# Keys and values from f16 parts of the context, and the query bias in one product, in a four-layer cross-attention kernel

## The chip, the cores and the metric

The kernel runs on one core of a Trainium2 chip. Its time is the device time of one launch in microseconds (us), and a verdict compares the medians of several runs of both kernels on the same chip.

## What is computed

Eight batches of 100 queries of width 128 go through four layers in turn. Layers 0, 1 and 3 are cross-attention of the queries over the same context of 1444 rows of width 128 (16 heads of 8 columns); layer 2 is causal attention over the first 100 context rows with a feed-forward behind it. Cut to what matters:

```python
# layer 0 (context first normalised by rows and scaled by gkv), layers 1 and 3 alike but with biases
q = (x @ Wq + bq).reshape(B, 100, 16, 8)
k = (ctx @ Wk + bk).reshape(B, 1444, 16, 8)
v = (ctx @ Wv + bv).reshape(B, 1444, 16, 8)
p = softmax(einsum('bshd,bkhd->bhsk', q, k) / sqrt(8))
x = norm(residual + einsum('bhsk,bkhd->bshd', p, v) ...)
```

Layer 0 has no bias of the queries; layers 1, 2 and 3 have one. All inputs are f32.

## The kernel before

**Units and stages.** A unit is one layer of 0, 1, 3 for one batch: 24 units, in the order layer 0 batches 0 to 7, layer 1, layer 3. The program is a pipeline of stages, and in stage n five units are at work: unit n+3 is loaded (`load`), the keys and queries of unit n+2 are made (`prep`), unit n+1 has its values made and the maxima of its scores taken (`top`), unit n has its exponentials and their products with the values (`exp`), and unit n-1 is finished (`post`). Layer 2 of a batch is done in the stages in which layer 3 of the same batch is `load` (attention, `att2`) and `prep` (feed-forward, `ff2`). `Unit.par` is the batch modulo 2, the half of a double buffer.

**Steps.** A stage has 48 steps j, one for each of 12 chunks of 120 or 121 context rows times 4 groups of heads. In each step TensorE makes one score product for the exponentials (L689, f16, 400 columns, into one of three `sexp` banks), one for the maxima (L650, the same shape, into one of four `ring` banks), and every four steps the products of four steps of probabilities with the values (L709). ScalarE takes the exponential (L957), VectorE the running maximum (L1081; L1079 for a first chunk). Every other piece of work is placed at a fixed step by the table `AT`: context transposes ct0 to ct2 at 0, 3, 6 (layer 0 alone), keys k0 to k2 at 9, 12, 15, queries at 19, values v0 to v2 at 22, 24, 26, mask transposes at 28, 30, 32, transposes of the maxima at 36 and 37. Each takes a ring bank in turn, so TensorE waits when the bank's last content hasn't been read. Every engine works strictly in its own written order.

**The work around the change.** `ctf` holds the transposed context in f32, [128, 2, 1444], one half for each parity. In layer 0 TensorE transposes the normalised rows (L577) and ScalarE scales and copies them into `ctf` (L890); in layers 1 and 3 SyncE loads a transposed copy of the context into it (L369), once the values of the unit that used this half are made. The keys are one f32 product of 480 or 484 columns for each of three groups (L588, `wk` stationary), read twice by ScalarE (L903: `kf` in f32, and the high part of `kp` in f16), and GpSimd subtracts the two for the low part (L476). The values are four f32 products of 128 columns in each of three groups (L596, `ctf` stationary, 120 or 121 columns of weights, `wv` moving), copied by ScalarE (L914). The queries are four f32 products of 100 columns (L622), and for layers 1 and 3 each is followed by a product of one row, `bq` with a row of ones, that adds the bias (L624). ScalarE then rounds them to f16 (L945), VectorE makes the parts (L1068), and GpSimd spreads them over heads (L503).

**GpSimd's order** in a stage: `spread2` of layer 2 (L487), three low parts of the keys (L476), `root` (L482), squares of a loaded context (L512, layer 0), `spread` (L503), the normalising of the loaded context (L519, L523, layer 0), and layer 2's `less_maximum` (L494) and `root`.

## Time and profile before

| | |
|---|---|
| median of 3 runs | 1166.34 us (1160.42 to 1167.5) |
| the profiled execution, its own time | 1159.32 us |
| its span, first to last instruction | 1157.5 us |
| busy: TensorE, VectorE, ScalarE, GpSimd | 1054.8, 812.2, 761.9, 292.2 us |
| mean granted TensorE clock | 0.95 of 2.4 GHz |

The span is what the profile's views divide; the profiled execution's own time is 1.8 us longer. Busy time of TensorE (PE) is modelled with overlapping ends, so what a matmul costs is read from the chain of work, where each piece has the time until the next could start; PEld is the loading of weights. DVE is VectorE, ACT ScalarE, POOL GpSimd, SPq the queue that issues DMAs.

### The profile page before, as it was taken

Reading aid. Unit: us, or ns where it says so; the run is one execution under the profiler, and the core shown is the slowest. Engines: PE = TensorE matmul, PEld = TensorE weight load, DVE = VectorE, ACT = ScalarE, POOL = GpSimd, SP = SyncE. Lnnn points to the kernel's source line nnn. Section 1 sums busy time; section 2 is a strip of 40 time slices with the busy share of each in tenths; the row PEclk is TensorE's granted clock in tenths of the full one; section 3 lists DMA queues with packets and bytes.
Section 4 is the critical chain, followed back from the end, with each engine's and each line's share of the span. In section 5 each row is a group of like instructions: output and inputs, shape, how many; then the busy total and the mean of one; then the engine's idle time right before and its main releaser. Section 6 shows DMA issues by size and latency. Waiting matters only on the chain.

```text
span 1157.5 us, 24776 instructions
## 1 busy us (share of the span) xinstructions
PE 1054.8 (91%) x9410; PEld 597.1 (52%) x9410; DVE 812.2 (70%) x1681; ACT 761.9 (66%) x1692; POOL 292.2 (25%) x267
## 2 busy tenths in 40 slices
PE   2689999999899999999999999999989999999996
PEld 1345555555455555555555555555555555564542
DVE  5787778768657767777876667676767777766851
ACT  1266776677577776867774666666666666756676
POOL 5644333532121122012113040404040313221100
PEclk9779999999999999999998899989899989998999
DMA  7421321221222222222231211112120202121100
GB/s 201 107 73 53 85 74 51 66 78 44 80 65 76 72 78 67 76 70 81 77 84 43 66 40 56 45 50 65 31 74 24 80 18 80 34 63 52 29 4 4
DMA packets 64350, 72.81 MB, mean 63 GB/s; under 512 B 8187, under 2 KB 59899, under 8 KB 64104
## 3 DMA queue, kind: packets, MB, share of 16 engines
q1 hardware_dynamic: 64232, 71.22, 21.6%
q8 instruction: 76, 1.25, 0.4%
q14 instruction: 42, 0.34, 0.1%
HBM read 50.25 MB, written 18.15 MB: 59 GB/s over the span
## 4 chain that ended last, share of the span: by engine, by line
PE 68%; DVE 16%; ACT 8%; issue 4%; SPq 1%; POOL 1%; DMA 0%; ACTq 0%; POOLq 0%; DVEq 0%
PE acc L709 17%; PE ring L650 15%; PE sexp L689 15%; PE ring L596 5%; PE ring L588 4%; DVE mx L1081 4%; DVE mneg L1087 4%; DVE mx L1079 3%; PE ring L622 2%; ACT probs L957 2%; PE ring L624 2%; PE ring L773 2%; ACT kp L903 2%; SPq L457 1%; PE ring L577 1%
## 5 line engine op out<-in xcount | busy, mean ns | idle before, releaser
L1081 DVE TENSOR_TENSOR mx<-ring,mx 120x400 f16<-120x400 f32 (+1 forms) x1056 | 556.2, 568 | 220.6 <-PE ring L650 217.3
L957 ACT ACTIVATE probs<-sexp 120x400 f32<-120x400 f32 (+1 forms) x1152 | 540.7, 514 | 191.5 <-PE sexp L689 186.6
L650 PE MATMUL ring<-qx,krep 96*128 96x400 f16 (+2 forms) x1152 | 399.1, 351 | 38.6 <-ACT kp L903 14.2
L689 PE MATMUL sexp<-qx,krep 97*128 97x400 f16 (+2 forms) x1152 | 396.3, 348 | 8.2 <-ACT probs L957 4.5
L709 PE MATMUL acc<-probs,vx 120*18 120x200 f32 (+1 forms) x4608 | 262.6, 347 | 0.8 <-ACT probs L957 0.7
L689 PEld LDWEIGHTS sexp<-qx,krep 97*128 97x128 f16 (+2 forms) x1152 | 126.3, 111 | 150.0 <-ACT probs L957 84.8
L650 PEld LDWEIGHTS ring<-qx,krep 96*128 96x128 f16 (+2 forms) x1152 | 128.5, 112 | 133.9 <-DVE mx L1081 31.0
L476 POOL TENSOR_TENSOR kp<-kf,kp 128x480 f16<-128x480 f32 (+1 forms) x72 | 80.9, 1130 | 357.3 <-ACT kp L903 357.3
L709 PEld LDWEIGHTS acc<-probs,vx 120*18 120x18 f32 (+1 forms) x4608 | 108.7, 99 | 118.6 <-issue 84.1
L503 POOL TENSOR_TENSOR qx<-qs,headmask 96x400 f16<-96x400 f16 x96 | 79.9, 862 | 78.7 <-DVE qs L1068 44.0
L914 ACT COPY vx<-ring 120x512 f32<-120x512 f32 (+1 forms) x72 | 42.3, 587 | 68.2 <-PE ring L596 68.2
L596 PE MATMUL ring<-wv,ctf 128*120 128x128 f32 (+1 forms) x576 | 81.3, 285 | 0.6 <-DVE qs L1068 0.6
L596 PEld LDWEIGHTS ring<-wv,ctf 128*120 128x120 f32 (+1 forms) x576 | 71.3, 187 | 19.8 <-issue 11.5
L588 PE MATMUL ring<-ctf,wk 128*128 128x484 f32 (+1 forms) x144 | 74.2, 600 | 4.2 <-ACT kp L903 2.4
L482 POOL TENSOR_TENSOR rstd<-vare,half 100x1 f32<-100x1 f32 x24 | 13.0, 541 | 215.1 <-DVE vare L1098 215.1
L1079 DVE CAST mx<-ring 121x400 f16<-121x400 f32 x96 | 52.2, 567 | 11.8 <-PE ring L650 11.8
L487 POOL TENSOR_TENSOR kbd<-k,heads 128x1600 f32<-128x1600 f32 x8 | 22.9, 2864 | 141.5 <-ACT v L978 141.5
L1087 DVE TENSOR_REDUCE mneg<-ring 100x8 f16<-100x968 f16 x48 | 55.4, 1156 | 0.9 <-PE ring L665 0.9
L1068 DVE SCALAR_TENSOR_TENSOR qs<-qh,headmask,ring 96x400 f16<-96x400 f16 x24 | 15.0, 627 | 47.6 <-ACT qh L945 47.6
L903 ACT ACTIVATE kf<-ring,cols 128x480 f32<-128x480 f32 (+1 forms) x48 | 31.9, 665 | 12.1 <-PE ring L588 12.1
L945 ACT CAST qh<-ring 96x400 f16<-96x400 f32 x24 | 11.7, 487 | 40.5 <-PE ring L624 36.5
L577 PE MATMUL ring<-ident,nat 120*128 120x120 f32 (+1 forms) x96 | 16.9, 312 | 20.4 <-DMA causal<-in_causal 20.4
(123 smaller groups left out, 924.3 us busy)
## 6 DMA issues: line engine op xcount, KB each, us to landing
krep<-kept SPq DMA_DIRECT2D x144, 120.0 KB, 2.6
ctf<-in_ctxT SPq DMA_DIRECT2D x16, 722.0 KB
kept<-kp SPq DMA_DIRECT2D x48, 240.0 KB, 2.8
krep<-kept SPq DMA_DIRECT2D x72, 121.0 KB, 2.8
kept<-kp SPq DMA_DIRECT2D x24, 242.0 KB, 2.5
nat<-in_ctx SPq DMA_DIRECT2D x8, 720.0 KB
maskexp<-maskmax SPq DMA_DIRECT2D x8, 281.2 KB, 3.4
anymask<-in_mask SPq DMA_DIRECT2D x1, 1128.1 KB, 6.8
```

Of the source, the lines that this page charges most:

```text
L476: pool.tensor_tensor(dst[:, 1, c0:c0 + n], src[:, c0:c0 + n], dst[:, 0, c0:c0 + n], ALU.subtract).then_inc(sem[done], 1)
L503: last = pool.tensor_tensor(qx[0:PARTS, u.third, t, :, :], qs[:, t, :].unsqueeze(1).broadcast_to([PARTS, HT, S]), headmask16[:, :].unsquee ...
L588: pe.matmul(ps[:, 0:n], wk[:, u.L, :], ctf[:, u.par, c0:c0 + n], start=True, stop=True).then_inc(sem["k_filled"], 1)
L596: last = pe.matmul(ps[0:r, D * i:D * i + D], ctf[:, u.par, c0:c0 + r], wv[:, u.L, :], start=True, stop=True)
L650: last = pe.matmul(ps[0:n, 0:QW], krep[0:PARTS, u.par, t, c0:c0 + n], qx[0:PARTS, u.third, t, :, :].rearrange("p f s -> p (f s)"), start=T ...
L689: last = pe.matmul(ps[0:n, 0:QW], krep[:, u.par, t, c0:c0 + n], qx[:, u.third, t, :, :].rearrange("p f s -> p (f s)"), start=True, stop=no ...
L709: last = pe.matmul(acc[32 * q:32 * q + VW, 2 * S * side:2 * S * side + 2 * S], vx[0:r, u.par, PAIRS * c + 2 * t + p, :], probs[0:r, j % PR ...
L903: op = act.activation(dst, src, ACT.Identity, bias=cols[:, bk:bk + 1]) if u.L else act.copy(dst, src)
L957: act.activation(probs[0:r, j % PR, :], sexp[j % SR][0:r, 0:QW], ACT.Exp).then_inc(sem["probs_ready"], 1)
L1079: op = dve.tensor_copy(dst, src)
L1081: op = dve.tensor_tensor(dst, src, dst, ALU.max)
L1087: dve.tensor_reduce(mneg[:, 8 * i:8 * i + 8], bank(f"mt{i}", u)[0:S, :].bitcast(F16).rearrange("s (h n) -> s h n", h=8)[:, :, 0:chunk(0)[1 ...
```

## The change

`ctf` becomes a single buffer [128, 1444]. A new tile `ct` [128, 2, 2, 1444] in f16 holds, for each parity, the high and the low part of the transposed context. GpSimd makes them, three groups per unit, ahead of everything else that it does in a stage: a copy f32 to f16, a wait for it, and a subtraction. Keys become three f16 products for each group (high by high, high weight by low context, low weight by high context), values three for each chunk, each product with its own load of weights. `wk` and `wv` are split once, by VectorE, at the start. The bias of the queries is one f16 product of 400 columns and 36 rows ahead of the four f32 products, which accumulate onto it. The load of the transposed context now waits for the last low part of the unit in `prep`, instead of the values of the unit in `top`. One more constant is loaded (`which`, [36, 401]), and `bq` grows from 1 to 36 rows.

```diff
-        bq = sb("bq", [1, 4, T * PARTS])
-        ones_row = sb("ones_row", [1, S])
+        bq = sb("bq", [32 + T, 4, PARTS])
+        bq16 = sb("bq16", [32 + T, 4, PARTS], F16)
+        which = sb("which", [32 + T, QW + 1])
+        which16 = sb("which16", [32 + T, QW], F16)
...
-        ctf = sb("ctf", [128, 2, KEYS])
+        ctf = sb("ctf", [128, KEYS])
+        ct = sb("ct", [128, 2, 2, KEYS], F16)
...
             def load_transposed(u, before):
 
-                sp.wait_ge(*at("v_filled", before, 3))
-                sp.dma_start(ctf[:, u.par, :], ctxT_in[u.batch]).then_inc(sem["ctx_loaded"], 16)
+                sp.wait_ge(*at("ct_low", before, 3))
+                sp.dma_start(ctf[:, :], ctxT_in[u.batch]).then_inc(sem["ctx_loaded"], 16)
...
                 if s.load is not None and s.load.L:
-                    load_transposed(s.load, s.top)
+                    load_transposed(s.load, s.prep)
...
+            def context(u, g, before):
+
+                _, c0, n, _ = groups()[g]
+                pool.wait_ge(*(at("ct_read", u, g + 1) if u.L == 0 else at("ctx_loaded", u, 16)))
+                if g == 0 and before is not None:
+                    pool.wait_ge(*at("v_filled", before, 3))
+                pool.tensor_copy(ct[:, u.par, 0, c0:c0 + n], ctf[:, c0:c0 + n]).then_inc(sem["ct_high"], 1)
+                pool.wait_ge(*at("ct_high", u, g + 1))
+                pool.tensor_tensor(ct[:, u.par, 1, c0:c0 + n], ctf[:, c0:c0 + n], ct[:, u.par, 0, c0:c0 + n], ALU.subtract
+                                   ).then_inc(sem["ct_low"], 1)
...
             def stage(s, n):
+                if s.prep is not None:
+                    for g in range(3):
+                        context(s.prep, g, s.exp)
                 if s.att2 is not None:
                     spread2(s.att2)
...
             def keys(u, g):
 
-                if u.L == 0:
-                    pe.wait_ge(*at("ct_read", u, g + 1))
-                elif g == 0:
-                    pe.wait_ge(*at("ctx_loaded", u, 16))
+                if u is UNITS[0] and g == 0:
+                    pe.wait_ge(sem["wk_ready"], 1)
+                pe.wait_ge(*at("ct_low", u, g + 1))
                 ps = begin(f"k{g}", u)
                 _, c0, n, _ = groups()[g]
-                pe.matmul(ps[:, 0:n], wk[:, u.L, :], ctf[:, u.par, c0:c0 + n], start=True, stop=True
-                          ).then_inc(sem["k_filled"], 1)
+                for j, (w, c) in enumerate(((0, 0), (0, 1), (1, 0))):
+                    last = pe.matmul(ps[:, 0:n], wk16[:, w, u.L, :], ct[:, u.par, c, c0:c0 + n], start=(j == 0),
+                                     stop=(j == 2))
+                last.then_inc(sem["k_filled"], 1)
 
             def vals(u, g):
 
+                if u is UNITS[0] and g == 0:
+                    pe.wait_ge(sem["rest_ready"], 1)
                 ps = begin(f"v{g}", u)
                 for i, c in enumerate(groups()[g][0]):
                     c0, r = chunk(c)
-                    last = pe.matmul(ps[0:r, D * i:D * i + D], ctf[:, u.par, c0:c0 + r], wv[:, u.L, :], start=True, stop=True)
+                    for j, (w, p) in enumerate(((0, 0), (1, 0), (0, 1))):
+                        last = pe.matmul(ps[0:r, D * i:D * i + D], ct[:, u.par, p, c0:c0 + r], wv16[:, w, u.L, :],
+                                         start=(j == 0), stop=(j == 2))
                 last.then_inc(sem["v_filled"], 1)
...
                 ps = begin("q", u)
+                if u.L:
+                    pe.matmul(ps[0:PARTS, 0:T * S], bq16[:, u.L, :], which16[:, :], start=True, stop=False, skip_group_check=True)
                 for t in range(T):
-                    last = pe.matmul(ps[0:PARTS, S * t:S * t + S], wq[:, u.L, t, :], xT[:, :], start=True, stop=not u.L)
-                    if u.L:
-                        last = pe.matmul(ps[0:PARTS, S * t:S * t + S], bq[0:1, u.L, PARTS * t:PARTS * t + PARTS], ones_row[0:1, :],
-                                         start=False, stop=True)
+                    last = pe.matmul(ps[0:PARTS, S * t:S * t + S], wq[:, u.L, t, :], xT[:, :], start=not u.L, stop=True,
+                                     skip_group_check=u.L > 0)
                 last.then_inc(sem["q_filled"], 1)
...
                 if g == 0 and before is not None:
-                    act.wait_ge(*at("v_filled", before, 3))
-                act.mul(ctf[:, u.par, c0:c0 + n], bank(f"ct{g}", u)[:, 0:n], cols[:, COLC["gkv"]:COLC["gkv"] + 1]
+                    act.wait_ge(*at("ct_low", before, 3))
+                act.mul(ctf[:, c0:c0 + n], bank(f"ct{g}", u)[:, 0:n], cols[:, COLC["gkv"]:COLC["gkv"] + 1]
                         ).then_inc(sem["ct_read"], 1)
...
+            def split(w, high, low):
+                step(dve.tensor_copy(high, w))
+                return dve.tensor_tensor(low, w, high, ALU.subtract)
+
+            split(wk[:, :, :], wk16[:, 0], wk16[:, 1]).then_inc(sem["wk_ready"], 1)
...
-            dve.tensor_scalar(bq[0:1, :, :], bq[0:1, :, :], SCALE, None, ALU.mult)
-            dve.memset(ones_row[0:1, :], 1.0)
+            step(dve.tensor_scalar(bq[:, :, :], bq[:, :, :], SCALE, None, ALU.mult))
+            step(dve.tensor_copy(bq16[:, :, :], bq[:, :, :]))
+            dve.scalar_tensor_tensor(out=bq16[:, :, :], in0=bq16[:, :, :], scalar=which[:, QW:QW + 1], in1=bq[:, :, :],
+                                     op0=ALU.mult, op1=ALU.add)
+            dve.tensor_copy(which16[:, :], which[:, 0:QW])
...
+            split(wv[:, :, :], wv16[:, 0], wv16[:, 1])
```

## Rows read from the trace of the kernel before

**Rows 1.** The page's chain that ended last, share by engine, then by line.
```profile
PE 68%; DVE 16%; ACT 8%; issue 4%; SPq 1%; POOL 1%; DMA 0%; ACTq 0%; POOLq 0%; DVEq 0%
PE acc L709 17%; PE ring L650 15%; PE sexp L689 15%; PE ring L596 5%; PE ring L588 4%; DVE mx L1081 4%; DVE mneg L1087 4%; DVE mx L1079 3%; PE ring L622 2%; ACT probs L957 2%; PE ring L624 2%; PE ring L773 2%; ACT kp L903 2%; SPq L457 1%; PE ring L577 1%
```
**Rows 2.** The chain in a layer-1 stage: start, length (us), engine, line.
```profile
533.62 0.81 PE ring L588 x2
...
535.51 0.56 ACT kp L903
...
537.75 0.17 PE ring L622 x2
537.93 0.34 PE ring L624 x2
538.26 0.34 PE ring L622 x2
...
542.25 1.06 PE ring L596 x8
...
543.48 0.17 PE ring L650
...
544.00 0.88 PE ring L596 x8
...
548.11 0.22 PE ring L605 x4
...
549.88 0.35 PE ring L605 x4
```
**Rows 3.** The chain in a layer-0 stage, at the queries.
```profile
132.38 0.69 PE ring L622 x8
```
**Rows 4.** The chain in a layer-3 stage.
```profile
672.33 0.56 ACT kp L903
...
674.98 0.88 PE ring L794 x8
...
693.73 1.06 PE ring L596 x8
```
**Rows 5.** Groups by line: count, busy us, mean ns, idle before and releasers.
```profile
L476 POOL TENSOR_TENSOR kp<-kf,kp 128x480 f16<-128x480 f32 (+1 forms) x72 | 80.9, 1130 | 357.3 <-ACT kp L903 357.3
L945 ACT CAST qh<-ring 96x400 f16<-96x400 f32 x24 | 11.7, 487 | 40.5 <-PE ring L624 36.5 <-PE ring L622 4.0
L605 PEld LDWEIGHTS ring<-identb,maskb 100*120 100x120 bf16 (+1 forms) x96 | 8.3, 134 | 4.4 <-issue 2.6 <-ACT maskmax L926 0.3
L1107 DVE TENSOR_TENSOR xall<-xn,rows 100x128 f32<-100x128 f32 x8 | 6.1, 759 | 0.3
L548 POOL MEMSET vx<- 128x1728 f32 x2 | 3.1, 1538 | 0.1
L1107 DVE TENSOR_TENSOR att<-xn,rows 100x128 f32<-100x128 f32 x8 | 2.3, 291 | 0.3
L1240 DVE TENSOR_TENSOR xall<-xall,rinvx 100x1024 f32<-100x1024 f32 x1 | 1.2, 1224 | 0.5 <-POOL rinvx L556 0.5
```
**Rows 6.** Windows: busy PE, PEld, DVE, ACT, POOL, then granted clock, DMA.
```profile
132.00:138.00 6.00, 6.00 (x56) 4.30 (x54) 3.79 (x8) 4.01 (x9) 5.99 (x6) 1.00 0.38 106
...
335.00:339.00 4.00, 4.00 (x29) 2.00 (x27) 2.07 (x4) 1.61 (x4) 2.89 (x4) 0.57 0.06 19
...
417.00:421.00 4.00, 4.00 (x38) 2.51 (x38) 2.13 (x5) 2.08 (x5) 2.11 (x3) 1.00 0.25 70
...
547.40:552.60 5.20, 5.20 (x62) 2.97 (x60) 4.00 (x8) 4.98 (x13) 0.00 (x0) 1.00 0.58 189
```
**Rows 7.** VectorE's maxima: duration ns min/median/max of all, starts.
```profile
L1081 DVE TENSOR_TENSOR mx<-ring,mx x1056: 556/565/579, 40.1 to 1116.2; 120x400 f16<-120x400 f32 x128, 121x400 f16<-121x400 f32 x48
```
**Rows 8.** GpSimd's timeline: start, length, instruction, count, idle before.
```profile
26.73 4.78 POOL L476 TENSOR_TENSOR kp<-kf,kp 128x484 f16<-128x484 f32 x3 [1.35 <-ACT kp L903]
...
711.82 0.54 POOL L482 TENSOR_TENSOR rstd<-vare,half 100x1 f32<-100x1 f32 x1 [16.83 <-DVE vare L1098]
```

More of the change, by code:

```diff
@@ L87, in rows_of, with build @@
         return tile[:, self.batch, :]
-def build(nc, ctx_in, ctxT_in, x_in, mask_in, w_qkv, w_o, w_1, w_2, rows_in, cols_in, bq_in, headmask_in, heads_in, ident_in,
-          causal_in, out):
+def build(nc, ctx_in, ctxT_in, x_in, mask_in, w_qkv, w_o, w_1, w_2, rows_in, cols_in, bq_in, which_in, headmask_in, heads_in,
+          ident_in, causal_in, out):
     with ExitStack() as es:
@@ L102, in build @@
         wv = sb("wv", [128, 4, D])
+        wk16 = sb("wk16", [128, 2, 4, D], F16)
+        wv16 = sb("wv16", [128, 2, 4, D], F16)
         wo = sb("wo", [128, 2, D])
@@ L191, in build @@
             "ctx_loaded": [32, 16, 0, 16], "row_power": [1, 0, 0, 0], "ctx_normal": [1, 0, 0, 0],
-            "ct_filled": [3, 0, 0, 0], "ct_read": [3, 0, 0, 0], "k_filled": G, "k_read": G, "k_lo": G,
+            "ct_filled": [3, 0, 0, 0], "ct_read": [3, 0, 0, 0], "ct_high": G, "ct_low": G, "k_filled": G, "k_read": G, "k_lo": G,
             "x_copied": one, "xT_filled": one, "xT_ready": one, "q_filled": one, "q_high": one,
@@ L217, in build @@
             PER[name] = [0, 0, per, 0]
-        setup_names = ["const_in", "pool_ready", "ones_ready", "acc_zero", "x_ready", "rest_ready", "x_power", "x_root", "setup",
+        setup_names = ["const_in", "pool_ready", "ones_ready", "acc_zero", "wk_ready", "x_ready", "rest_ready", "x_power", "x_root", "setup",
                        "mask_in_all", "mask_counted", "flag_filled", "flag_ready"]
@@ L454, in load_constants @@
                                  (w2[:, :, :], w_2.rearrange("(j f) n -> f j n", f=128)),
-                                 (bq[0:1, :, :], bq_in), (headmask[:, :], headmask_in), (heads[:, :], heads_in),
+                                 (bq[:, :, :], bq_in), (which[:, :], which_in), (headmask[:, :], headmask_in), (heads[:, :], heads_in),
                                  (causal[:, :], causal_in)):
@@ L866, in stage @@
                         flag_sum()
-            pe.wait_ge(sem["const_in"], 16 * 14)
+            pe.wait_ge(sem["const_in"], 16 * 15)
             pipeline(UNITS, stage, last=MASK_STAGES[0] - 1)
@@ L1007, in stage @@
                         if s.prep is not None and s.prep.L == 0 and j == AT[f"ct{g}"]:
-                            context(s.prep, g, s.exp)
+                            context(s.prep, g, s.top)
                         for part in range(2):
@@ L1035, in stage @@
                         act.copy(maskflag[:, :], bank("flag", None)[0:1, 0:1]).then_inc(sem["flag_ready"], 1)
-            act.wait_ge(sem["const_in"], 16 * 14)
+            act.wait_ge(sem["const_in"], 16 * 15)
             pipeline(UNITS, stage)
@@ L1276 @@
     zero = np.zeros(D, np.float32)
-    bq = copies(np.stack([zero, a["L1_xattn_bq"], a["L2_xattn_bq"], a["L3_xattn_bq"]])).reshape(1, 4, T * PARTS)
+    bq = np.zeros((32 + T, 4, PARTS), np.float32)
+    which = np.zeros((32 + T, QW + 1), np.float32)
+    for row in (0, 32):
+        bq[row:row + T] = copies(np.stack([zero, a["L1_xattn_bq"], a["L2_xattn_bq"], a["L3_xattn_bq"]])).transpose(1, 0, 2)
+        which[row:row + T, 0:QW] = np.repeat(np.eye(T), S, axis=1)
+    which[32:, QW] = -1.0
     headmask = np.zeros((PARTS, HT + 1), np.float32)
@@ L1287 @@
         "w_o": np.stack([a["L0_xattn_wo"].T, a["L1_xattn_Wo"].T]), "w_1": a["L2_xattn_W1"].T, "w_2": a["L2_xattn_W2"].T,
-        "rows": np.broadcast_to(rows, (S,) + rows.shape), "cols": cols, "bq": bq, "headmask": headmask, "heads": heads,
+        "rows": np.broadcast_to(rows, (S,) + rows.shape), "cols": cols, "bq": bq, "which": which, "headmask": headmask, "heads": heads,
         "ident": np.eye(128, dtype=np.float32)[None], "causal": causal,
```

2 lines of the change are left out of this document (1 added, 1 removed).

## Prediction

> **What bounds the kernel now.** I read the page first: TensorE is busy for 1054.8 of 1157.5 us, and it has 68% of the chain that ended last, against 16% for VectorE and 8% for ScalarE [rows 1]. The lines that the change touches, L588, L596, L622 and L624, hold 4, 5, 2 and 2% of that chain. So most of their work stands on the path, and a cut of them is worth something. The second view is the chain in single pieces, since a piece there has the time until the next could start: the reader is to see that keys, queries and values follow the score products without a gap, but for one at k2, where TensorE waits for ScalarE's L903 [rows 2]. The third view is the granted clock: 1.00 (2.4 GHz) in most stretches, 0.57 in 335 to 339 us, right behind the queries of a layer-1 unit [rows 6]. I found such a fall behind the queries of five layer-1 units (near 335, 376, 458, 499 and 580 us), none behind those of two others (one of them in 417 to 421 us), and none behind the queries of layer 0, whose four products have no bias product between them (132 to 138 us at 1.00).
>
> **Keys.** Now one f32 product of 480 columns takes 0.81 us [rows 2]. Afterwards there are three f16 products; a product of 400 f16 columns takes 0.17 us in that chain, 0.43 ns a column, so 3 x 480 columns take 0.61 us and a group saves 0.2. In layers 0 and 1 all three groups are on the chain: units 2 to 15 (the first two run before exponentials fill the stages), 14 x 3 x 0.195 = 8.2 us. In layer 3 the first group lies in a stretch that ScalarE bounds, with two table loads for layer 2's feed-forward up to its L903 at 672.33 [rows 4], so 8 x 2 x 0.195 = 3.1. Together 11.3 us less. Whether ScalarE can follow is charged below.
>
> **Values.** A group takes 1.06, 0.88 and 1.06 us: 16 passes of 128 columns are 0.88, and 0.18 more is the first load of weights where the products of L709 stand ahead [rows 2]. Afterwards a group is 12 f16 products of 128 columns. The disputed point is the load of 120 columns of weights for each of them. The nearest row is the mask's transposes, L605: 120 columns of 16-bit weights and 100 columns moving, four in 0.22 us, four in 0.35 where the first load is exposed [rows 2]. The loads are thus hidden down to 55 ns a product, which is what 128 columns need. A group is 12 x 0.055 = 0.66, with 0.13 for an exposed first load in two of three: 2.24 against 3.00 us, 0.76 less a unit. That three products accumulate in one place costs nothing extra by L794, where four f32 products (16 passes) accumulate in 0.88 us [rows 4]. In 15 units all groups are on the chain. In the 8 stages in which layer 2's attention runs, VectorE bounds the first two and only the third is on it (693.73 [rows 4]): 15 x 0.76 + 8 x 0.27 = 13.6 us less.
>
> The bounds of a product: 0.055 from L605, and 0.134 (the duration of its weight load, [rows 5]) + 0.055 = 0.19 if no load were hidden. I take the lower, since L605 differs only in being a transpose. The Trainium skill, TensorE: Matmul & The Clock Gate, section LDWEIGHTS, has a load take P / 1.2 ns for P columns, which would be an estimated 0.10 us for 120 and more than the columns need. The fours in 0.22 us speak against it.
>
> **Queries.** In layers 1 and 3 the block is 0.17 + 7 x 0.34 = 2.55 us: each one-row bias product costs 0.34 and holds the next product at 0.34 too [rows 2]. Without them four products take 0.69 us [rows 3]. Afterwards: 0.69 + one f16 product of 400 columns at 0.17 = 0.86, so 1.69 less for each of 16 units, 27.0 us. ScalarE's L945 waits 36.5 / 16 = 2.3 us for these products [rows 5], more than 1.69, so nothing of ScalarE's is next in line within the saving; VectorE waits for L945 in turn. This is the largest and surest term.
>
> **The clock behind the queries.** A fall lasts 3.4 us by the windows' shares (0.43 x 2 x 4.0 [rows 6]), in which TensorE does half its work: 1.7 us lost. The five falls go if the one-row products are what lets the clock fall; layer 0 says so. 5 x 1.7 = 8.5 us less; at worst 0.
>
> **GpSimd's new work.** For each unit three copies and three subtractions. A subtraction has the form of L476, 1.1 us [rows 5]. A copy has no row: between 0.43 (484 elements at the pace of the memset L548, 1728 in 1.54) and 1.17 (two inputs, L476); I take 0.8, the middle. A group is 1.9 us, a unit 5.7, GpSimd some 430 instead of 292 us busy. The Trainium skill, GPSIMD Engine Reference, section 4.1, calls one-input operations roughly line-rate; by that a copy would be near my lower end and the start below a microsecond cheaper. In a layer-3 stage GpSimd comes to it after `root` at 711.82 [rows 8] and ends near 718, with the first group at 714.3. `root` waits for work of step 41, and k0 stands 16 steps later, at step 9 of the next stage; 24 stages of 48 steps in 1157.5 us make a step about 1 us, so k0 is due a good 10 us behind `root`. What is queued behind the new work (L487, L476) waits for things that come later still. In layers 0 and 1 it ends earlier still: in layer 0 ct0 to ct2 stand at steps 0, 3, 6 and k0 to k2 at 9, 12, 15, a lead of 7 us over a group of 1.9. So in a full stage it costs nothing. If the cover were gone, keys would wait, with a whole unit's 5.7 us as the price.
>
> It costs at the **start**, where GpSimd is the chain: it goes from the first L476 at 26.73 straight on to the first `spread` [rows 8]. 5.7 us come in front, and VectorE's split of `wk` (2 x 0.6, from L1240's 1.22 for 1024 [rows 5]) delays what GpSimd does ahead; 1.35 us of GpSimd's idle time and some of the 4.78 us, in which three operations of 1.1 lay beside VectorE's, are won back. I charge 4 us (2 to 7), constants included.
>
> It costs by the shared way to memory. VectorE's L1107 with both inputs in SBUF takes 0.759 us beside GpSimd's work and 0.291 without [rows 5]. After `root` of layer 2 the scaling (two such operations) will meet the new work: 8 x 0.25 = 2 us (0 to 8). The maxima, with one input in PSUM, take 556 to 579 ns all through the trace, beside GpSimd or not [rows 7], and stay as they are. (By this the trace agrees with the Trainium skill, GPSIMD Engine Reference, section 1: contention with VectorE's instructions that have two SBUF inputs.)
>
> **Moved wait.** SyncE's load of the context waits for a low part that is long made and goes out near step 17 instead of 26. It stands ahead of the second replication (step 32) as before, so nothing queued behind it waits longer. No cost, no gain.
>
> **ScalarE next.** In the masks' stretch of a layer-1 stage it is busy for 4.98 of 5.2 us [rows 6]; there it will lag, and I charge 8 x 0.3 = 2.5 us (0 to 8).
>
> **Sum.** -11.3 - 13.6 - 27.0 - 8.5 + 4 + 2 + 2.5 = -52 us. On the profiled execution's own 1159.3 that is 1107; it lies 7 us below the median of the runs, 1166.3, which would give 1114. The runs lie on both sides, so I put the time at 1111 us, 4.7% below the median.
>
> **Rivals.**
> *Other engines take the gain.* VectorE has a maximum of 0.57 us in every step [rows 7] and ScalarE little room left beside masks; if behind each shortened block one of them holds, half of keys and values goes (12.5), and if the clock falls just as often, the 8.5 too: -52 + 21 = -31, 1128 to 1135. For it speaks the 4.98 of 5.2 us [rows 6]; against it that TensorE's products follow each other without a gap [rows 2].
> *Loads of 16-bit weights set the pace of the values*, at 0.10 us a product: a group is 1.2 instead of 1.0, so 15 x 0.6 + 8 x 0.2 = +10.6 instead of -13.6: -28, 1138 on the median. The skill's section LDWEIGHTS gives this price.
> *Slower: no load is hidden.* 0.19 us a product: 53 groups on the chain x (2.28 - 1.0) = +68, keys 58 x 0.13 = +8 instead of -11.3, no clock gain for lack of dense work, queries -27, the rest +8.5: +57, about 1220. It decides from about 0.14 us a product, where 636 products lose what queries and keys gain. L605's rows speak against it.
> *It does not do what it says*: the clock falls behind the queries stay since their cause is the wait at k2 ahead of them. That alone is 8.5 us and inside my range.
>
> **How the numbers follow.** Forecast 0.73; other engines 0.14; weight loads 0.06; none hidden 0.03; something at the start or in the clock that eats nearly all 0.04. The forecast's own range is 1096 to 1126: all terms at their best and two more falls gone, or the charges at their upper ends. The rivals' 1128 to 1138 come in up to 1136. A difference under about 1% can't be told from none by a measurement here. So faster by over 1%: 0.92; within: 0.05; slower: 0.03.
>
> **What would show it.** L588 three pieces in 0.62 us in place of 0.81; L596 twelve in 0.66 to 0.79; L624 one piece of 0.17 with L622's four in 0.69; no clock below 1.00 behind layer 1's queries; GpSimd near 430 us, done before k0 in each stage; GpSimd's first L476 near 32 us instead of 26.73. A layer-1 stage gets some 3 us shorter and more where a clock fall goes, a layer-0 stage 1.3. Wrong would make it: TensorE waiting for `ct_low` at k0, L596 at over 1 us, or VectorE's chain growing by what TensorE's loses.

## The result and the profile after

| | before | after |
|---|---|---|
| median of 4 runs each, same chip | 1163.8 us (1160.42 to 1167.5) | 1117.8 us (1113.61 to 1119.82) |
| the profiled execution, its own time | 1159.32 us | 1119.34 us |
| its span | 1157.5 us | 1117.6 us |
| mean granted TensorE clock | 0.95 | 0.96 |

The ratio is 0.9599, with a 95% interval of 0.9573 to 0.9625: 4.0% faster. That is 46 us between the medians and 40 us between the two profiled executions; the profiled one of after lies at the upper end of its runs (0.960 mean clock, where the fastest, 1113.61 us, had 0.966), and the profiled one of before, 1159.32, lies below all its four runs. So the traces compared below show some 6 us less gain than the medians.

The page's chain by engine and by line, of the changed kernel, to be held against [rows 1]:

```profile
PE 62%; DVE 21%; ACT 8%; issue 5%; POOL 2%; SPq 1%; DMA 0%; POOLq 0%; ACTq 0%; DVEq 0%
PE acc L733 16%; PE ring L674 15%; PE sexp L713 14%; DVE mx L1105 6%; DVE mneg L1111 4%; DVE mx L1103 3%; PE ring L607 3%; PE ring L619 3%; ACT probs L981 2%; PE ring L797 2%; ACT kp L927 2%; PE ring L648 2%; DVE max L1206 1%; SPq L462 1%; ACT sc L1006 1%
```

TensorE's share fell from 68 to 62% and VectorE's rose from 16 to 21%. The keys (L588, now L607) went from 4 to 3% and the values (L596, now L619) from 5 to 3%; the bias, 2% as L624, has left the list. Where TensorE gave time up, VectorE's maximum (L1081, now L1105) took some of it over.

The chain of after in a layer-1 stage, beside [rows 2]; columns are start, length (us), engine, line:

```profile
508.43 0.57 DVE mx L1105
...
511.66 0.61 PE ring L607 x3
...
518.43 0.30 PE ring L646
518.73 0.87 PE ring L648 x8
519.63 0.50 ACT qh L969
...
520.15 0.63 DVE qs L1092
520.77 1.45 DVE mx L1105 x3
522.22 0.59 DVE xn L1129
...
525.35 0.81 PE ring L619 x12
```

Keys and values are as forecast: three key products in 0.61 us where one f32 product took 0.81, and twelve value products in 0.81 where four f32 products took 1.06 (x8 in the view, which has two passes for each f32 product). The query block is shorter but not as short: 0.30 + 0.87 = 1.17 us instead of 0.17 + 0.69 = 0.86. Behind it stand ScalarE's rounding and VectorE's work (519.6 to 524.2), which in the kernel before ran beside TensorE's longer value products (542.25 on in [rows 2]).

A layer-0 stage of after, the same view, beside [rows 3]:

```profile
165.68 0.57 DVE mx L1105
...
166.48 0.37 DVE oatt L1146 x2
...
168.92 0.61 PE ring L607 x3
...
171.75 0.62 PE ring L607 x3
...
175.50 0.69 PE ring L648 x8
...
178.02 0.82 PE ring L619 x12
...
179.53 0.67 PE ring L619 x12
...
181.69 0.81 PE ring L619 x12
```

The first of the three key groups is not on the chain here: it runs beside VectorE's maximum and output step (L1143, L1146), which end later. In the kernel before all three stood on the chain, in layer 0 and in layer 1; of a layer-1 stage of before:

```profile
567.42 0.81 PE ring L588 x2
...
570.37 0.81 PE ring L588 x2
...
573.40 0.81 PE ring L588 x2
```

In after the values sum to 2.30 us (2.24 forecast, 3.00 before).

Windows of after, one behind a layer-1 query block and one in layer 3 (PE, PEld, DVE, ACT, POOL, granted clock, DMA):

```profile
519.00:523.00 4.00, 4.00 (x50) 2.68 (x49) 2.87 (x7) 2.40 (x6) 2.08 (x3) 1.00 0.77 183
...
697.00:701.00 4.00, 3.87 (x16) 2.60 (x17) 1.15 (x2) 3.12 (x9) 3.31 (x2) 0.57 0.02 4
```

Behind the queries of a layer-1 unit (519 to 523 us) the clock stays at 1.00, as it does at the places that answer to the five falls of before. But it falls at 697 to 701 us, in layer 3, right behind a wait of TensorE for ScalarE, and again behind the waits at the same place of three later stages, at 806, 966 and 1021 us. The kernel before has one such fall, at 728 us, behind this wait:

```profile
727.29 0.28 PE L726 MATMUL ring<-ident,oatt 100*128 100x100 f32 x1 [1.28 <-ACT kp L903]
```

Groups of after, by line: the new work of GpSimd, the values' loads, and ScalarE's reading of the queries, which is L945 of [rows 5]:

```profile
L492 POOL TENSOR_TENSOR ct<-ctf,ct 128x480 f16<-128x480 f32 (+1 forms) x72 | 81.4, 1131 | 5.8
...
L490 POOL CAST ct<-ctf 128x480 f16<-128x480 f32 (+1 forms) x72 | 44.7, 621 | 57.8 <-ACT ctf L914 41.9
L619 PEld LDWEIGHTS ring<-wv,ct 128*120 128x120 f16 (+1 forms) x864 | 55.6, 133 | 19.2 <-issue 8.9
...
L969 ACT CAST qh<-ring 96x400 f16<-96x400 f32 x24 | 11.7, 488 | 16.6 <-PE ring L648 16.6
```

ScalarE waited 40.5 us in all for the queries before and waits 16.6 us now: (40.5 - 16.6) / 16 = 1.49 us less per unit. GpSimd is busy for 414.7 us (292.2 before).

**Where the time went.** The distance from one stage's first transpose of the negated maxima (L673, now L697) to the next one's is a stage's length. In us:

| stretch | before | after | difference | by the prediction's terms |
|---|---|---|---|---|
| up to the first such transpose (start) | 72.89 | 78.97 | +6.1 | +4 |
| stages 0 to 5 (keys of layer 0) | 234.7 | 228.2 | -6.5 | -8.1 |
| stage 6 (layer 1's first queries) | 45.9 | 41.9 | -4.0 | -4.4, a fall with it |
| stages 7 to 12 (layer 1) | 245.3 | 224.7 | -20.6 | -23.2, of it -6.8 for four falls |
| stage 13 (layer 1's last queries) | 55.6 | 50.0 | -5.6 | -2.7 |
| stages 14 to 22 (layer 3) | 465.4 | 455.7 | -9.8 | -16.8 |
| the rest | 37.7 | 38.1 | +0.4 | 0 |
| span | 1157.5 | 1117.6 | -39.9 | -51 of the -52 |

The last column takes the forecast's terms by the units whose keys, values and queries fall in the stretch. Most of what is missing is in the last stretch but one; stage 13 had time at the lower clock of 12.0 us before and 1.8 after, which no term of mine held.

A stage of layer 1 without a fall of the clock went from 39.78 to 37.41 us (-2.37); one with a fall had 41.34.

### The profile page after: what moved, and what is told of

Same layout as the page of the kernel before. It is cut to its first block, busy times and chain, and to the rows that moved or that the text cites. A ratio compares the mean times of both kernels' runs of the same rounds, so it can differ in the third digit from the quotient of the medians.

```text
span 1117.6 us, 25480 instructions
## 1 busy us (share of the span) xinstructions
PE 1000.5 (90%) x9658; PEld 554.8 (50%) x9658; DVE 818.8 (73%) x1687; ACT 762.0 (68%) x1692; POOL 414.7 (37%) x411
## 4 chain that ended last, share of the span: by engine, by line
PE 62%; DVE 21%; ACT 8%; issue 5%; POOL 2%; SPq 1%; DMA 0%; POOLq 0%; ACTq 0%; DVEq 0%
PE acc L733 16%; PE ring L674 15%; PE sexp L713 14%; DVE mx L1105 6%; DVE mneg L1111 4%; DVE mx L1103 3%; PE ring L607 3%; PE ring L619 3%; ACT probs L981 2%; PE ring L797 2%; ACT kp L927 2%; PE ring L648 2%; DVE max L1206 1%; SPq L462 1%; ACT sc L1006 1%
## 5 line engine op out<-in xcount | busy, mean ns | idle before, releaser
L1105 DVE TENSOR_TENSOR mx<-ring,mx 120x400 f16<-120x400 f32 (+1 forms) x1056 | 554.5, 567 | 197.0 <-PE ring L674 194.7
L674 PE MATMUL ring<-qx,krep 96*128 96x400 f16 (+2 forms) x1152 | 398.7, 351 | 43.0 <-ACT kp L927 14.6
L733 PE MATMUL acc<-probs,vx 120*18 120x200 f32 (+1 forms) x4608 | 258.7, 343 | 0.8 <-ACT probs L981 0.7
L674 PEld LDWEIGHTS ring<-qx,krep 96*128 96x128 f16 (+2 forms) x1152 | 127.7, 111 | 128.1 <-DVE mx L1105 30.9
L481 POOL TENSOR_TENSOR kp<-kf,kp 128x480 f16<-128x480 f32 (+1 forms) x72 | 79.4, 1108 | 204.6 <-ACT kp L927 204.6
L519 POOL TENSOR_TENSOR qx<-qs,headmask 96x400 f16<-96x400 f16 x96 | 80.1, 864 | 54.1 <-PE sexp L713 30.3
L492 POOL TENSOR_TENSOR ct<-ctf,ct 128x480 f16<-128x480 f32 (+1 forms) x72 | 81.4, 1131 | 5.8
L607 PE MATMUL ring<-ct,wk 128*128 128x480 f16 (+1 forms) x216 | 59.6, 386 | 12.8 <-POOL ct L492 9.1
L490 POOL CAST ct<-ctf 128x480 f16<-128x480 f32 (+1 forms) x72 | 44.7, 621 | 57.8 <-ACT ctf L914 41.9
L619 PEld LDWEIGHTS ring<-wv,ct 128*120 128x120 f16 (+1 forms) x864 | 55.6, 133 | 19.2 <-issue 8.9
L619 PE MATMUL ring<-wv,ct 128*120 128x128 f16 (+1 forms) x864 | 62.4, 222 | 0.8 <-DVE qs L1092 0.7
L607 PEld LDWEIGHTS ring<-ct,wk 128*128 128x128 f16 x216 | 20.2, 99 | 35.7 <-issue 18.5
```

Source lines behind the costliest of these rows:

```text
L481: pool.tensor_tensor(dst[:, 1, c0:c0 + n], src[:, c0:c0 + n], dst[:, 0, c0:c0 + n], ALU.subtract).then_inc(sem[done], 1)
L492: pool.tensor_tensor(ct[:, u.par, 1, c0:c0 + n], ctf[:, c0:c0 + n], ct[:, u.par, 0, c0:c0 + n], ALU.subtract).then_inc(sem["ct_low"], 1)
L519: last = pool.tensor_tensor(qx[0:PARTS, u.third, t, :, :], qs[:, t, :].unsqueeze(1).broadcast_to([PARTS, HT, S]), headmask16[:, :].unsquee ...
L607: last = pe.matmul(ps[:, 0:n], wk16[:, w, u.L, :], ct[:, u.par, c, c0:c0 + n], start=(j == 0), stop=(j == 2))
L619: last = pe.matmul(ps[0:r, D * i:D * i + D], ct[:, u.par, p, c0:c0 + r], wv16[:, w, u.L, :], start=(j == 0), stop=(j == 2))
L674: last = pe.matmul(ps[0:n, 0:QW], krep[0:PARTS, u.par, t, c0:c0 + n], qx[0:PARTS, u.third, t, :, :].rearrange("p f s -> p (f s)"), start=T ...
```

## The experiments

All ran beside the kernel before on the same chip, whose medians there were 1163.53 us (e1 to e4), 1163.12 (e5 to e8) and 1162.27 (e9, e10). Ratios are to these, with 95% intervals.

**e1: the bias alone.** The kernel before, with the constants and the bias product of the change, keys and values as they were.

```diff
                 ps = begin("q", u)
+                if u.L:
+                    pe.matmul(ps[0:PARTS, 0:T * S], bq16[:, u.L, :], which16[:, :], start=True, stop=False, skip_group_check=True)
                 for t in range(T):
-                    last = pe.matmul(..., wq[:, u.L, t, :], xT[:, :], start=True, stop=not u.L)
-                    if u.L:
-                        last = pe.matmul(..., bq[0:1, u.L, PARTS * t:PARTS * t + PARTS], ones_row[0:1, :], start=False, stop=True)
+                    last = pe.matmul(..., wq[:, u.L, t, :], xT[:, :], start=not u.L, stop=True, skip_group_check=u.L > 0)
```

> The kernel before with the bias product alone changed: one f16 product of 400 columns ahead of the four f32 products. My theory: the queries' block of layers 1 and 3 falls from 2.55 to 0.86 us, 16 x 1.69 = 27 us, and the falls of TensorE's clock behind the queries of layer 1 go, 5 x 1.7 = 8.5 us: 35 us less than before, about 1129 us, with the start where it was (first L650 near 38 us). Rival, the clock falls come from TensorE's wait at k2 and stay: 27 us less, 1137, and windows behind layer 1's queries still at half clock. Rival, the saving of the whole change comes mostly from keys and values: under 20 us less.

Measured: 1127.72 us (1125.43 to 1129.35), ratio 0.9691 (0.9668 to 0.9714), 36 us less. A layer-1 stage takes 38.27 to 38.56 us, 1.51 less than the undisturbed 39.78, and the clock doesn't fall behind a layer-1 query block. Its chain there:

```profile
524.90 0.30 PE ring L624
525.19 0.86 PE ring L626 x8
```

L624 is the bias and L626 the four query products in this kernel. So about three quarters of the change's gain is this one edit.

**e2: keys and values alone.** The changed kernel with the old bias, four one-row f32 products each behind its query product.

```diff
-                if u.L:
-                    pe.matmul(ps[0:PARTS, 0:T * S], bq16[:, u.L, :], which16[:, :], start=True, ...)
                 for t in range(T):
                     last = pe.matmul(..., wq[:, u.L, t, :], xT[:, :], start=True, stop=not u.L)
+                    if u.L:
+                        last = pe.matmul(..., bq[0:1, u.L, PARTS * t:PARTS * t + PARTS], ones_row[0:1, :], start=False, stop=True)
```

> The changed kernel with the old bias: four one-row f32 products between the four f32 products of the queries. My theory: keys and values give 11 + 14 us by the sum, the start takes 6 to 7 (it was measured at 6.1 to the first stage's end in the changed kernel), so 15 to 20 us less than before, about 1146 us, and falls of the clock behind layer 1's queries are back. Rival, keys and values as f16 products are most of the gain: 1130 or less. Rival, they gain nothing on the whole once the start is paid: 1160 to 1166.

Measured: 1147.62 us (1144.01 to 1151.49), ratio 0.9851 (0.9824 to 0.9879), 16 us less. Chain and windows of e2; L646 are the one-row products, L644 the queries, and the window of 4 us is the one behind them:

```profile
530.36 0.34 PE ring L646 x2
530.70 0.34 PE ring L644 x2
```

```profile
532.50:536.50 4.00, 4.00 (x29) 1.62 (x29) 3.17 (x6) 1.95 (x4) 2.43 (x3) 0.57 0.79 245
```

The block is as long as before, and the clock falls behind the queries of five layer-1 units again. A stage without a fall takes 38.92, one with it 40.5 us: a fall costs 1.6 us. In an undisturbed layer-1 stage the two halves add up exactly: -1.51 (e1) and -0.86 (e2) make the -2.37 of the whole change. The medians don't add up so well: 36 and 16 us against 46. The profiled executions do (spans shorter by 32.6 and 7.8 us, against 39.9).

**e3: same products, other order.** The kernel before, the four one-row products together ahead of the four query products. Arithmetic and products are the same ones.

```diff
+                if u.L:
+                    for t in range(T):
+                        pe.matmul(..., bq[0:1, u.L, PARTS * t:PARTS * t + PARTS], ones_row[0:1, :], start=(t == 0), stop=False, ...)
                 for t in range(T):
-                    last = pe.matmul(..., wq[:, u.L, t, :], xT[:, :], start=True, stop=not u.L)
-                    if u.L:
-                        last = pe.matmul(..., bq[0:1, ...], ones_row[0:1, :], start=False, stop=True)
+                    last = pe.matmul(..., wq[:, u.L, t, :], xT[:, :], start=not u.L, stop=True, ...)
```

> The kernel before with its four one-row f32 bias products in front of the four products of the queries instead of between them; same products, same count. If it is the alternation of one-row and 128-row products that costs 0.34 us for each of them, the block is 8 x 0.17 = 1.4 us instead of 2.55, 16 x 1.15 = 18 us less, about 1145. If a one-row f32 product itself takes 0.34, the block is 4 x 0.34 + 0.69 = 2.05, 8 us less, 1156. If one-row products are also what lets the clock fall, the falls behind layer 1's queries get fewer with the shorter block; if they come from the wait at k2, they stay.

Measured: 1138.41 us (1131.99 to 1140.96), ratio 0.979 (0.9767 to 0.9812), 25 us less, by order alone. The chain of e3, L623 the one-row products and L626 the queries, and the window behind them:

```profile
526.62 0.85 PE ring L623 x8
527.47 0.86 PE ring L626 x8
```

```profile
528.50:532.50 4.00, 4.00 (x41) 2.84 (x39) 3.58 (x7) 2.78 (x7) 2.84 (x4) 1.00 0.36 95
```

Eight passes of one row take 0.85 us, as many as eight of 128 rows: a one-row product is not dear in itself. The block falls from 2.55 to 1.71 us, and the score product behind it from 0.28 to 0.17, since TensorE now changes twice between one row and many instead of eight times (the eighth change is the one out of the block); (2.55 + 0.11 - 1.71) / 6 = 0.16 us a change, and a layer-1 stage is 0.95 us shorter (39.78 to 38.83). And no clock falls behind it any more, with all four one-row products there. So what lets the clock fall is the alternation (or the long block of half-idle passes that it makes), not one-row products as such.

**e8: the bias product over 128 rows.** The changed kernel; 92 rows of zeros are added, so that all products of the block have 128 rows. The score product ahead of it has 96. Two more memsets at the start.

```diff
-        bq16 = sb("bq16", [32 + T, 4, PARTS], F16)
-        which16 = sb("which16", [32 + T, QW], F16)
+        bq16 = sb("bq16", [128, 4, PARTS], F16)
+        which16 = sb("which16", [128, QW], F16)
```

> The changed kernel with the bias product widened from 36 to 128 rows, the added ones zero. Its block was 0.30 + 0.87 = 1.17 us in the profile, where 0.17 + 0.69 were forecast. If a change of the row count between products costs 0.13 to 0.17 us, as the run with the bias products in front suggests (its two rows of four are 0.85 and 0.86 instead of 0.69 each), the block is now 0.86 to 0.9, 16 x 0.3 = 5 us less, 1113 us. Rival, the accumulation onto the 400 columns costs it: no change, 1117 to 1118.

Measured: 1112.82 us (1111.17 to 1115.55), ratio 0.9572 (0.9543 to 0.9601). An undisturbed layer-1 stage goes from 37.41 to 37.12 us. The chain of e8:

```profile
517.68 0.17 PE ring L646
517.85 0.70 PE ring L648 x8
```

0.17 + 0.70 = 0.87 us instead of 0.30 + 0.87 = 1.17: with 3.6 times the rows the same 400 columns cost 0.30 us less, and the block now is what I had forecast. 16 units x 0.30 = 4.8 us, and the medians differ by 5.0; the intervals of the two ratios overlap, so the verdict rests on the chain and the stage. Not every other count of rows costs: from the 96 rows of the score product (L674) to the 128 of this bias product it is 0.17 us for 400 columns, as among score products.

What the price consists of stays open. TensorE's timeline, first of the changed kernel, then of e8 (PEld is the load of weights):

```profile
518.37 0.37 PE L646 MATMUL ring<-which,bq 36*96 36x400 f16 x1
518.66 0.76 PEld L648 LDWEIGHTS ring<-xT,wq 128*96 128x96 f32 x8 [0.18 <-issue]
```

```profile
517.52 0.33 PE L646 MATMUL ring<-which,bq 128*96 128x400 f16 x1
517.52 0.85 PEld L648 LDWEIGHTS ring<-xT,wq 128*96 128x96 f32 x8
```

In e8 the first load for the queries starts together with the bias product and is hidden by it; behind 36 rows it starts only with its own product, 0.29 us later. So a change may cost because a load is no longer hidden, or because TensorE empties first; no run separates the two. The Trainium skill, TensorEngine Tiling (Array Packing), section Key Properties, says that changing the tiling mode drains TensorE. If a product of 1 or 36 rows is run as a smaller tile, this could be that drain; the traces show 0.13 to 0.17 us for a change into or between the products of the block, and not the mode.

**e4: GpSimd's new work twice.** Each copy and each subtraction is done a second time, with a wait between.

```diff
                 pool.tensor_copy(ct[:, u.par, 0, c0:c0 + n], ctf[:, c0:c0 + n]).then_inc(sem["ct_high"], 1)
+                pool.tensor_copy(ct[:, u.par, 0, c0:c0 + n], ctf[:, c0:c0 + n]).then_inc(sem["twice"], 1)
+                pool.wait_ge(*at("twice", u, 2 * g + 1))
...
+                pool.tensor_tensor(ct[:, u.par, 1, c0:c0 + n], ...).then_inc(sem["twice"], 1)
+                pool.wait_ge(*at("twice", u, 2 * g + 2))
```

> The changed kernel with each of GpSimd's copies and subtractions for the context made twice, 5.1 us more of its time for a unit, 122 us in all. If the new work is hidden in full stages, as I hold, only the start pays: 5 to 8 us more than the changed kernel, 1123 to 1126 us, the periods of layer-0 and layer-1 stages as in the changed kernel (38.4 and 37.4 us). Rival, GpSimd's work slows VectorE or delays keys in full stages and so took part of the gain in layer 3: 15 us more or over, 1133 and up, with longer layer-3 stages.

Measured: 1127.34 us (1126.34 to 1129.42), ratio 0.9689 (0.9671 to 0.971), 9.5 us more than the changed kernel. The first stage's transpose comes at 91.04 instead of 78.97 us (+12.1), and the stages of layers 0 and 1 are as long as in the changed kernel (38.38 and 37.41). In a full stage GpSimd has that much room: the whole cost of the new work is at the start. Stages 14 to 22 take 449.8 us here against 455.7 in the changed kernel, with 51 us at the lower clock in stages 14 to 21 against 66; so GpSimd's work isn't what holds layer 3 up, and layer 3's time differs by some 6 us between two kernels whose TensorE does the same there.

**e5: the start in another order.** GpSimd makes unit 0's context parts ahead of the root for the queries (L575), and VectorE splits `wv` before it waits for that root.

```diff
+                if n == -2:                      # behind the context parts of unit 0
+                    pool.wait_ge(sem["x_power"], 1)
+                    pool.tensor_tensor(rinvx[:, :], ssqx[:, :], half[0:S, 0:B], ALU.pow).then_inc(sem["x_root"], 1)
...
-            pool.wait_ge(sem["x_power"], 1)
-            pool.tensor_tensor(rinvx[:, :], ssqx[:, :], half[0:S, 0:B], ALU.pow).then_inc(sem["x_root"], 1)
```

> The changed kernel with the start in another order: GpSimd makes unit 0's context parts before the root of the queries' norm, and VectorE splits the value weights while it waits for that root. My theory: the 6 to 7 us that the start costs come from GpSimd's copies standing behind a root that waits for VectorE, and from both engines' operations on SBUF in each other's way; about 3 to 4 us are won back, the first L674 at 41 to 42 us instead of 45.25, the total near 1114 us. Rival: the two engines' contention is all of it, and the order only moves it: no difference, 1117 to 1118.

Measured: 1118.97 us (1116.69 to 1119.13), ratio 0.9619 (0.9595 to 0.9644): no gain; my theory fell. GpSimd's timeline in the changed kernel, then the chain in e5 (in the timeline: start, length, instruction, idle before and what ended it):

```profile
24.80 2.27 POOL L575 TENSOR_TENSOR rinvx<-ssqx,half 100x8 f32<-100x8 f32 x1 [2.82 <-DVE ssqx L1264]
27.03 2.17 POOL L490 CAST ct<-ctf 128x484 f16<-128x484 f32 x1
29.27 2.29 POOL L492 TENSOR_TENSOR ct<-ctf,ct 128x484 f16<-128x484 f32 x1
...
33.68 0.59 POOL L490 CAST ct<-ctf 128x480 f16<-128x480 f32 x1
34.34 1.10 POOL L492 TENSOR_TENSOR ct<-ctf,ct 128x480 f16<-128x480 f32 x1
```

```profile
29.85 1.43 POOL ct L492
31.28 2.05 POOL rinvx L549
...
33.36 2.12 DVE xall L1275
...
35.50 2.01 DVE xall L1276
...
37.53 0.30 ACT xcur L960
```

The parts are ready at 31.3 us instead of 35.4, four us earlier, as I had meant. But now the root is late, with it VectorE's two operations on `xall` (2.1 and 2.0 us beside GpSimd's work, 1.2 and 1.5 in the changed kernel), and ScalarE has the copy of `xcur` written ahead of its reading of the third key group; so the third low part (L481) starts at 38.83 us against 38.01. Two chains meet at the start, and what is taken from one is put on the other.

**e6 and e7: work for TensorE in layer 2's attention.** 5 (e6) or 13 (e7) f16 products of 368 columns per stage, into unused columns, among the products of nine columns (L797). They compute nothing that is read.

```diff
+                for _ in range({0: 4, 1: 3, 2: 3, 3: 3}[t]):     # e7; e6: 2, 1, 1, 1
+                    pe.matmul(ps[0:S, 144:512], ident16[:, 0:S], wk16[:, 0].rearrange("p l d -> p (l d)")[:, 0:368], start=True, stop=True)
```

> The changed kernel with five useless f16 products of 368 columns (into unused columns of the bank) between the products of 9 columns of layer 2 (L797), 8 x 5 x 0.16 = 6.3 us more work of TensorE. If those sparse products are what lets the clock fall behind them in layer-3 stages (20 windows of 3.4 us at half clock in the profile, 1.7 us lost in each), half of the falls go and the time is 10 us lower, 1108 us or less for the fillers' cost included. Rival, the clock doesn't hang on them, or five are too few: the fillers cost what they take, 1122 to 1124 us.

> As the kernel with five fillers, but thirteen of them, 8 x 13 x 0.16 = 16.6 us more work. If the density of TensorE's work there decides, the falls behind L797 are gone in all stages (12 to 14 windows, 20 to 24 us), and the time comes to 1110 to 1115; if it doesn't, 1132 to 1135.

Measured: e6 1121.37 us (median of three runs, 1120.32 to 1122.52; a fourth took 3168.36 and is left aside, with it the median is 1121.94), ratio 0.9651 (0.9621 to 0.968), mean clock 0.968. e7 1118.95 us (1115.6 to 1121.36), ratio 0.9619 (0.9587 to 0.965), mean clock 0.983. The time at the lower clock is 89.4 us in the changed kernel, 71.4 in e6 and 37.5 in e7, whose stages 14 to 18 take 54.04 to 54.23 us, with a fall in them or without. So the falls can be driven out, but not at a profit: the products are 104 x 0.16 = 16.6 us of work, and 51.9 us less at the lower clock give TensorE half of that back, 26 us; of the 9 us that should be left none arrives. In the chain from 735 to 790 us VectorE's maximum has 11.1% instead of 5.6%: with TensorE filled and at full clock, VectorE ends last in more places.

**e9: the gap behind the gelu filled.** The changed kernel, but in layer 3's k0 three more f16 products of the high parts stand ahead of the three real ones, whose first overwrites them.

```diff
+                for _ in range(3 * (u.L == 3 and g == 0)):
+                    pe.matmul(ps[:, 0:n], wk16[:, 0, u.L, :], ct[:, u.par, 0, c0:c0 + n], start=True, stop=True)
```

> The changed kernel, but in layer 3's k0 three f16 products of the high parts more, written into the bank ahead of the three real ones (0.61 us of work for TensorE in the stretch where it then waits 1.56 us for ScalarE's gelu and probabilities). Theory A: the new falls of the clock at 697, 806, 966 and 1021 us come since TensorE now idles longer there; with the gap filled they go, the added work is hidden by the wait, and the kernel gains 4 x 1.5 = 6 us: 1112. Theory B: the clock falls by what TensorE does over longer stretches or at random; the falls come elsewhere or stay, and the time stays at 1118 to 1119, with layer-3 stages as long as they are.

**e10: e8 and e9 together.**

> Both edits together: the bias product over 128 rows, 92 of them zero, and the three products more in layer 3's k0. The bias product alone gave 5 us. Theory A: both add up, 1107 to 1108. Theory B: the padding gives nothing, 1112 to 1114.

Measured: e9 1113.76 us (1111.53 to 1115.25), ratio 0.9578 (0.9548 to 0.9607); e10 1109.23 us (1107.66 to 1113.37), ratio 0.9546 (0.9518 to 0.9574), the fastest of all. TensorE's timeline at the gap, of the changed kernel and of e9:

```profile
697.13 0.40 PE L750 MATMUL ring<-ident,oatt 100*128 100x100 f32 x1 [1.56 <-ACT kp L927]
```

```profile
699.84 0.28 PE L752 MATMUL ring<-ident,oatt 100*128 100x100 f32 x1 [0.94 <-ACT kp L929]
```

and the window right behind it in e9, to be held against 697 to 701 us above:

```profile
699.80:703.80 4.00, 3.96 (x36) 2.48 (x37) 2.08 (x5) 3.46 (x10) 3.40 (x2) 1.00 0.00 0
```

In stages 14 to 16 the gap is 1.28 us in the kernel before, 1.56 in the changed one, since three f16 products fill 0.2 us less of the time ahead of it than one f32 product, and 0.94 in e9. In the later stages it is shorter: 1.02, 1.13 and under 0.7 in stages 17 to 20. The clock fell behind it at 697, 806, 966 and 1021 us in the changed kernel (waits of 1.56, 1.13, 1.13 and 1.05 us), not behind the same waits of the other four stages, and at none of these places in e9 or e10. The added 0.61 us is hidden by the wait for ScalarE.

The gain, 4.0 us over the changed kernel and 3.6 over e8, is less than the 6 I expected, and the intervals overlap. Nor are the falls surely the padding's doing: e4 and e5, whose gaps are as long as the changed kernel's, have one fall behind them each, e8 has three, and stages 14 to 22 take 449.8 and 452.7 us in e4 and e5, 449.6 in e9. So theory A is likely, as both padded kernels have no such fall and both are faster than their partners, but it isn't shown. (The other falls of layer 3, in the stretch of 9-column products, come in numbers that differ from run to run; the mean clock of e9's five runs is 0.963 to 0.968.)

## Why the prediction was right, and where its terms were off

The forecast was 1111 us, with a range of its own of 1096 to 1126; the median is 1117.8. The mechanism held: the path is TensorE's, the cuts of its products shorten it, and the query bias is the largest part. The size was 46 us between the medians instead of 52, and the range was wide enough to hold several terms that were off, most of them to the same side. By its own steps:

- **Keys**, -11.3 forecast. The size of a group was right (0.61 us, 0.2 less). The count was wrong: all three groups are on the chain of before in layers 0 and 1, as I had it, but in after k0 lies beside VectorE's L1105 and L1143 to L1146, which end last (165.68 and 508.43 us above). I had taken the chain of before for that of after. With two groups a unit the term is 14 x 2 x 0.195 + 3.1 = 8.6 us.
- **Values**, -13.6. A unit's three groups take 2.30 us (2.24 forecast). Twelve products with a load of 120 columns each take 0.67 us where the first load is hidden, 0.056 us a product, as L605 of [rows 2] had it. The two rivals in which loads set the pace are out. The Trainium skill, TensorE: Matmul & The Clock Gate, section LDWEIGHTS, has a load take P / 1.2 ns, an estimated 0.10 us for 120 columns. The trace has 0.133 us for a load (L619 above) and 0.056 us for a product, so loads overlap, and the length of a load isn't the pace.
- Keys and values together gave 1.10 us in a layer-0 stage (39.48 to 38.38) and 0.86 in a layer-1 stage (e2) instead of 1.35.
- **Queries**, -27.0, 1.69 a unit. Measured 1.51 (e1) and 1.49 (L969's waits), 24 us. What failed is the price of the bias product, "one f16 product of 400 columns at 0.17": it costs 0.30, and the first query product behind it 0.17 more, since its 36 rows stand among products of 96 and 128 rows (e3, e8). My row for 0.17 was a score product among others of its own shape. The rows for it stood in [rows 2]: 0.34 at each change between L622 and L624, where the same passes follow each other at 0.17 without one.
- **The clock behind the queries**, -8.5. Five falls of the eight units are gone, at 1.6 us each, 8 us. The reason I gave, the one-row products, is only half true: in e3 all of them are there and the clock stays up. It is their alternation with the others, or the longer block that this makes.
- **Start**, +4. It is +6.1 at the first stage. The copy is 0.59 us at its steady pace, below my 0.8. The Trainium skill, GPSIMD Engine Reference, section 4.1, calls one-input operations roughly line-rate; my lower end of 0.43 was a little nearer to the measured 0.59 than my 0.8. But at the start the first copy took 2.17 and the first subtraction 2.29 us, beside VectorE's two-input operations at 27.5 to 30.3 us: 8.4 us for three groups, where a layer-1 stage takes 5.2 (413.8 to 419.0 us), and the first low part of the keys comes at 35.4 instead of "near 32". Doubled work costs 12 us there and nothing elsewhere (e4), and the order can't mend it (e5).
- **SBUF contention of VectorE**, +2. The scaling behind layer 2's `root` did meet the new work, as said. Its second operation, of 0.29 us in [rows 5], became dearer than I had it:

```profile
L1131 DVE TENSOR_TENSOR att<-xn,rows x8: 553/1078/1082, 630.0 to 1008.0; 100x128 f32<-100x128 f32 x8
```

  It is 0.8 us longer in seven of the eight stages and 0.26 in the eighth. But only the first of the eight, at 630 us, stands on the chain; in the others the chain there is TensorE's, and VectorE idles again a few steps on.
- **ScalarE next in layer 1**, +2.5. About right in size: keys and values gave 0.24 us less in a layer-1 stage than in a layer-0 stage, where I had charged 0.3. And ScalarE does lag beside the masks: in stages 6 to 8 its mask work is on the chain, where it wasn't before, for example

```profile
412.28 1.40 ACT maskb L944
...
414.43 0.55 ACT probs L981
```

  In stages 9 to 12, hardly different in length, it is VectorE's work behind the queries instead.
- **Layer 3** is where most of the gap to the forecast lies, and no term of mine is the one that failed there. Of the 12 us between the forecast's -52 and the -40 of the profiled pair, 7 are in stages 14 to 22. The seven full ones among them became 1.06 us shorter on the mean, where the terms gave 2.35 less charges of 0.25. Their pieces did get shorter; but the time at the lower clock in stages 14 to 21 rose from 49 to 66 us, five falls more, about 8 us. e2 alone gave nothing at all in these seven stages (386.4 us against 385.4 before), e1 alone 9.3 us. I had counted clock falls as a gain only; that the clock could fall more often in layer 3, no step of mine held. One cause is likely: shortening k0 lengthens a wait of TensorE's for ScalarE, and behind it stand four falls in the changed kernel and one in the kernel before. But e4 and e5, with the same wait, have one each, so it isn't shown. The time at the lower clock in stages 14 to 21 is 49 to 51 us in the three kernels with f32 keys (before, e1, e3), 61 to 68 in the changed kernel, e2, e5 and e8, but 51 in e4, and 47 to 55 with the padding (e9, e10).
- **The rival "other engines take the gain"** had part of the truth: VectorE took over k0's saving in layers 0 and 1, and it or ScalarE a further 0.24 us in a layer-1 stage.

What stays open: why the number of falls in layer 3, behind the wait and in the stretch of the 9-column products, differs between kernels that do the same there. In the four runs of the changed kernel the time goes with the mean clock (1119.82 us at 0.960, 1113.61 at 0.966), so it probably sets most of their spread.

## What to carry to other kernels

Price a product by its neighbours: in this kernel a product with few rows between full ones costs two changes, and zero rows that make it full can be cheaper than leaving them out; first try to order like products together. Cutting work in front of a wait for another engine saves nothing, and it may cost clock, so look at what the clock does behind each wait that the cut makes longer. A chain of before says what is on the path before; a cut changes which engine ends last, so name the engine behind each cut piece. Work moved to an idle engine was free here in the full pipeline only; its price was the start, beside everything else that is done there once.

## What the runs showed of the hardware

- A change between a product of 1 or 36 rows and one of 96 to 128 costs TensorE 0.11 to 0.17 us, at each change (e3: 0.16 on the mean; e8: 0.30 for two). A change between 96 and 128 rows costs nothing (e8: 0.17 us for 400 columns). Eight passes of one row take 0.85 us, eight of 128 rows 0.86 (e3).
- 16-bit loads of 120 columns, 0.133 us each, hide down to 0.056 us a product, in chains of twelve with three products accumulating in one place.
- GpSimd's copy of 128x484 from f32 to f16 takes 0.59 us in a full stage and 2.17 beside VectorE's operations with two SBUF inputs; VectorE's subtraction L1257 of 128x512 takes 0.69 us beside GpSimd's memsets (`wk`) and 1.47 beside its copy and subtraction (`wv`). Both sides pay.
- In the changed kernel's layer 3 the granted clock fell to its lower level behind waits of TensorE of 1.56, 1.13, 1.13 and 1.05 us and stayed at the upper one behind the same waits of four other stages; the length of the wait alone doesn't decide it.
